# Moving weight pieces, a level table and a few waits in a hand-ordered attention and mixture-of-experts kernel

## The chip, the cores and the metric

The kernel runs on one core of one Trainium2 chip. The metric is the device time of one execution in microseconds (us). A core has five engines that run their own instruction streams and meet only at semaphores: TensorE (PE), VectorE (DVE), ScalarE (ACT), GpSimd (POOL) and SyncE (SP), which here only issues DMAs.

## The reference, cut to what matters

16 batches of 256 tokens of width 256. Each batch goes through a cross attention (16 heads of 16, queries from the normalised `x`, keys and values from a context), and then through a feed-forward part: one shared expert that all tokens take, and two routed experts of which each token takes one with its full weights and the other as a constant level, since an expert that is not chosen sees a zero token.

```
x = x + xattn(layernorm(x), ctx, ctx, Wq, Wk, Wv, Wo)       # x: (16, 256, 256)
x = x + ffn(layernorm(x), gate_w, w1, b1, w2, b2, sw1, sb1, sw2, sb2)

# xattn, for each 64x64 block pair (r, c) with |r - c| <= 3; here 4 blocks of queries and 4 of keys
scores = q_r @ k_c.T * 16 ** -0.5
out_r += softmax(scores) @ v_c                              # a softmax for each block pair, then summed
# ffn, f = layernorm(x)
e = argmax(f @ gate_w.T)                                    # 2 routed experts, hidden width 1024
routing = sum over n of relu((f if n == e else 0) @ w1[n] + b1[n]) @ w2[n] + b2[n]
shared  = relu(f @ sw1 + sb1) @ sw2 + sb2
```

## The kernel before, in words

**Batches and stages.** `iteration(i)` is the same function on every engine. It does the attention of batch `i`, the shared expert of batch `n = i - 1` (called S below, with hidden units u0 to u3: `shared_up`, `shared_down`), and one tile of 256 routed tokens, tile `m = i - 2` (`tile_up`, `tile_down`). Iterations 0, 1 and 2 have no tile yet (`tile` is false), iteration 0 has no shared part. Iterations 4 to 13 or 14 are a loop; after iteration 15 a tail finishes tile 14, the shared part of batch 15, tile 15 (called `last`) and two left-over tiles. Products in full precision are made of a high and a low half of each operand: ACT writes the high half (`..._hi`), DVE or POOL subtracts for the low half (`..._lo`), and PE runs three products.

**Inside an iteration, PE.** Four `visit`s compute scores for row maxima (DVE's `maximum`, line 1176); `maxima` transposes these (line 604) for the shift of the softmax, which SP carries through DRAM into `QP` (`shift`). Then come the next batch's projections: k (from the context's `c_hi`, `c_lo`), the transposes of its tokens, and q. ACT and DVE write q and k into `T`, SP stores them in DRAM (`bounces`) and loads them spread over heads into `KP` and `QP` (`spread`, 24 DMAs in two halves). Eight pairs of heads follow: `scores_t` (line 622), ACT's exponentials, `values` (line 638), and DVE's `divide` (lines 1187 to 1197), which writes `T` and counts `t_done`. `divide` of pair 0 waits until q and k have left `T`. `attention_out` (line 652) sums the blocks; its first half needs pairs 0 to 3 and its second pairs 4 to 7. `visit(i + 1, 0)` (line 589), `project_out` (line 666, result added to the residual `x1` by DVE line 1203), `front_v` (v of the next batch) and `prep_tokens` (line 542, after the second layer norm) end the iteration.

**Weights.** The raw weights of the experts come in 24 pieces of 256 KB, loaded by POOL into 5 staging buffers (`stage`, which lie in buffers that are free in the beginning, two of them `h32`). ACT writes the high half of a piece (`split_high`, line 960), POOL the low half (`split_low`, line 1537) and then loads the next piece that uses this buffer. `SPLITS_AT` says how many pieces are split at each of the numbered places of iteration 0. Pieces 0 to 7 are the shared expert's, 8 to 23 the routed ones'. PE waits for all 24 before iteration 1. `table(e)`, in iterations 1 and 2, computes the constant level of expert `e` out of the whole of it: 24 products.

**Order.** Every engine's order is that of the code. SP is a queue too: a DMA that waits holds back all DMAs behind it. `load_residual(i)` waits for `y_done`, which DVE raises in the middle of the divides (iterations 1 and 2) or at their start (later), and it stands ahead of `spread`.

## Time and profile before

| what | value |
|---|---|
| median of 3 runs | 916.06 us (911.68 to 916.23) |
| the profiled execution, its own time | 914.49 us |
| span of its trace (first to last instruction) | 912.7 us |
| PE busy | 798.9 us (88%) |
| DVE, ACT, POOL busy | 593.8, 497.3, 429.5 us |
| mean granted TensorE clock | 0.954 of full speed |

The span is 1.8 us shorter than the execution's own time. Busy time is an average over very different stages. In the stretch of the weight pieces PE has gaps and runs at a low clock; in the loop it is nearly always busy. In the rows below, a number in square brackets is the idle time of the engine just before the instruction, with what ended it.

### The profile page before, as it was taken

Reading aid. Unit: us, or ns where it says so; the run is one execution under the profiler, and the core shown is the slowest. Engines: PE = TensorE matmul, PEld = TensorE weight load, DVE = VectorE, ACT = ScalarE, POOL = GpSimd, SP = SyncE. Lnnn points to the kernel's source line nnn. Section 1 sums busy time; section 2 is a strip of 40 time slices with the busy share of each in tenths; the row PEclk is TensorE's granted clock in tenths of the full one; section 3 lists DMA queues with packets and bytes.
Section 4 is the critical chain, followed back from the end, with each engine's and each line's share of the span. In section 5 each row is a group of like instructions: output and inputs, shape, how many; then the busy total and the mean of one; then the engine's idle time right before and its main releaser. Section 6 shows DMA issues by size and latency. Waiting matters only on the chain.

```text
span 912.7 us, 24404 instructions
## 1 busy us (share of the span) xinstructions
PE 798.9 (88%) x8374; PEld 665.8 (73%) x8374; DVE 593.8 (65%) x1248; ACT 497.3 (54%) x1150; POOL 429.5 (47%) x780
## 2 busy tenths in 40 slices
PE   3465777788999999999999999999999999989894
PEld 3333756577886869697878788787879697868794
DVE  4457577576757777685858676767677686745331
ACT  2264453636565575746575656556574756465452
POOL 2667333342536364554536363637364554455311
PEclk8576998999999999999999999999999999999997
DMA  6669221263624544544535353444444444414730
GB/s 193 185 194 304 69 86 35 81 206 96 199 79 123 161 138 144 159 141 140 170 115 196 114 166 125 145 140 136 161 128 151 149 144 136 148 49 140 239 109 23
DMA packets 97387, 128.19 MB, mean 140 GB/s; under 512 B 14655, under 2 KB 82623, under 8 KB 97088
## 3 DMA queue, kind: packets, MB, share of 16 engines
q1 hardware_dynamic: 89760, 107.89, 38.4%
q0 software_dynamic: 6624, 18.95, 6.2%
q10 hardware_dynamic: 960, 0.79, 0.4%
q8 instruction: 26, 0.43, 0.2%
q14 instruction: 17, 0.14, 0.1%
HBM read 90.80 MB, written 37.04 MB: 140 GB/s over the span
## 4 chain that ended last, share of the span: by engine, by line
PE 62%; DVE 14%; DMA 9%; issue 4%; ACT 4%; POOL 2%; SPq 2%; ACTq 1%; DVEq 0%; POOLq 0%
PE hid L533 16%; PE acc L724 14%; PE nd L638 11%; PE work L533 6%; PE work L622 5%; DVE nmax L1176 4%; PE work L666 3%; DVE PT L1219 2%; PE work L589 2%; DMA QP<-scratch_m 2%; DVE T L1192 2%; DVE check L1187 1%; DMA scratch_q<-T 1%; PE work L542 1%; DMA scratch_m<-mT 1%
## 5 line engine op out<-in xcount | busy, mean ns | idle before, releaser
L1442 POOL TENSOR_TENSOR hl<-h,hh 128x256 fp32r<-128x256 f32 x228 | 169.0, 744 | 326.1 <-ACT hh L982 325.9
L966 ACT ACTIVATE PT<-work 128x512 f32<-128x512 f32 x192 | 106.3, 605 | 55.6 <-PE work L622 55.5
L1195 DVE RECIPROCAL T<-nd 128x256 f32<-128x256 f32 x51 | 89.4, 1753 | 37.9 <-PE nd L638 32.8
L724 PE MATMUL acc<-w_hi,hh 128*128 128x256 f32 (+1 forms) x528 | 112.5, 295 | 0.0
L982 ACT ACTIVATE h<-hid,bias 128x256 f32<-128x256 f32 x144 | 69.1, 480 | 74.7 <-PE hid L533 74.7
L533 PE MATMUL hid<-Xs,W 128*128 128x256 f32 x816 | 109.6, 288 | 0.2
L533 PEld LDWEIGHTS hid<-Xs,W 128*128 128x128 f32 x816 | 102.9, 195 | 2.6 <-DVE Xs L1129 0.7
L724 PE MATMUL acc<-w_lo,hh 128*128 128x256 f32 (+1 forms) x528 | 104.7, 280 | 0.0
L533 PE MATMUL hid<-Xr,W 128*128 128x256 f32 x768 | 104.1, 285 | 0.0
L533 PEld LDWEIGHTS hid<-Xr,W 128*128 128x128 f32 x768 | 94.1, 188 | 5.1
L638 PE MATMUL nd<-PT,V 128*32 128x256 f32 x1024 | 84.0, 401 | 11.5 <-DVE T L1192 5.3
L1176 DVE TENSOR_REDUCE nmax<-work 128x8 f32<-128x512 f32 x128 | 82.3, 686 | 15.0 <-PE work L589 14.6
L724 PEld LDWEIGHTS acc<-w_hi,hh 128*128 128x128 f32 x528 | 80.6, 189 | 11.0 <-issue 7.0
L724 PE MATMUL acc<-w_hi,hl 128*128 128x256 f32 (+1 forms) x528 | 82.9, 279 | 0.0
L1176 DVE TENSOR_REDUCE nmax<-nd 128x8 f32<-128x512 f32 x128 | 82.8, 680 | 0.0
L724 PEld LDWEIGHTS acc<-w_lo,hh 128*128 128x128 f32 x528 | 81.0, 190 | 0.0
L638 PE MATMUL nd<-PT,bsum 128*32 128x256 f32 x1024 | 80.7, 387 | 0.0
L982 ACT ACTIVATE h<-hid,bsel 128x256 f32<-128x256 f32 x120 | 57.8, 481 | 41.1 <-PE hid L533 39.9
L622 PEld LDWEIGHTS work<-QP,KP 56*128 56x128 f32 x384 | 37.7, 188 | 50.7 <-issue 34.1
L724 PEld LDWEIGHTS acc<-w_hi,hl 128*128 128x128 f32 x528 | 70.9, 189 | 0.0
L982 ACT ACTIVATE hh<-hid,bias 128x256 fp32r<-128x256 f32 x144 | 69.4, 482 | 0.0
L622 PE MATMUL work<-QP,KP 56*128 56x256 f32 x384 | 61.4, 330 | 7.5 <-ACT hh L982 3.7
(191 smaller groups left out, 1651.5 us busy)
## 6 DMA issues: line engine op xcount, KB each, us to landing
W<-w1q SPq DMA_DIRECT2D x64, 512.0 KB, 5.8
KP<-scratch_k SPq DMA_DIRECT2D x192, 64.0 KB, 2.4
QP<-scratch_q SPq DMA_DIRECT2D x180, 64.0 KB, 2.3
scratch_k<-T SPq DMA_DIRECT2D x16, 512.0 KB, 3.5
scratch_q<-T SPq DMA_DIRECT2D x16, 512.0 KB, 3.2
yt<-yq SPq DMA_DIRECT2D x17, 260.0 KB, 2.8
xt<-xq SPq DMA_DIRECT2D x17, 256.0 KB, 3.8
xin<-x SPq DMA_DIRECT2D x16, 256.0 KB, 3.5
```

Source lines behind the costliest of these rows:

```text
L533: mm = nc.tensor.matmul(dst, R(s), R(m), start=n == 0, stop=n == len(steps) - 1)
L589: mm = nc.tensor.matmul(banks[s][:, SEQ * n:SEQ * n + SEQ], R(QP[rows, 2 * g + n, P * t:P * t + P]), R(KP[rows, 2 * g + n, :]), start=True ...
L622: mm = nc.tensor.matmul(banks[s][:, SEQ * t:SEQ * t + SEQ], R(KP[rows, p, P * t:P * t + P]), R(QP[rows, p, :]), start=True, stop=True)
L638: mm = nc.tensor.matmul(nd[r:r + 32, p % 2, kind, :], V[:, t, 2 * p + s, :] if kind == 0 else bsum[:, :], PT[:, (2 * p + s) % 4, t, :], st ...
L666: mm = nc.tensor.matmul(bank[:, D * t:D * t + D], R(part[:, c, P * t:P * t + P]), R(w[:, c, :]), start=first, stop=part is a_lo and c == D ...
L724: mm = nc.tensor.matmul(acc[:, t, :], R(h[:, u % 2, a, P * t:P * t + P]), R(row), start=first, stop=u == UNITS - 1 and h is hl and a == 1, ...
L966: nc.scalar.activation(PT[:, j % 4].rearrange("p t q -> p (t q)"), score_bank(j), ACT.Exp).then_inc(sem["exp_done"], 1)
L982: last = nc.scalar.activation(dst, hid[:, u % 2, a, :], ACT.Relu, bias=bias[:, 2 * u + a:2 * u + a + 1])
L1176: nc.vector.tensor_reduce(nmax[:, t, :].rearrange("q (b s p) -> q s p b", s=2, b=NBLK) [:, s, 2 * g:2 * g + 2, :], bank.rearrange("q (n b ...
L1192: nc.vector.scalar_tensor_tensor(out=T[:, p, :], in0=check[:, p % 2], scalar=2.0, in1=T[:, p, :], op0=ALU.add, op1=ALU.mult).then_inc(sem[ ...
L1195: nc.vector.reciprocal(T[:, p, :], nd[:, p % 2, 1, :]).then_inc(sem["inverted"], 1)
L1442: nc.gpsimd.tensor_tensor(R(hl[:, u % 2, a]), h32[:, u % 2, a], hh[:, u % 2, a], ALU.subtract).then_inc(sem["hl_done"], 1)
```

## The change

These things move, and nothing is computed differently:

1. `context_high(1)` and `context_low(1)` run ahead of the weight pieces, not behind the first four.
2. The split places become (4, 0, 0, 0, 0, 4, 2, 1, 1, 1, 1, 1, 1, 1, 1, 2, 0, 4), the last one in iteration 1. Pieces 20 to 23 are so split in iteration 1, between the shared expert's u1 and u2, and their buffers are 2, 3, 4 and again 3, since `h32` is in use by then. PE waits for pieces 6 and 7 before iteration 1, and for the last piece in `table(0)`.
3. DVE makes the low halves of pieces 5, 7 and 9.
4. `make_constants` goes from before the divides of iteration 0 to behind that of pair 3; `scores_t` of iteration 0 waits for the load of the constants only.
5. In iterations 0 to 2 the residual's load goes behind `spread`.
6. In iterations 1 and 2 `shared_up(n, 3)` goes ahead of the q projection, and `table` behind `front_v`.
7. Everywhere `ranks` goes behind `shared_down(n, 1)`. In iterations 3 to 15 the halves of `attention_out` are apart: the first ahead of `tile_down(m, 1)`, the second behind the first scores of the next batch.
8. Tail: the token load of tile `last` goes behind its second weight load, from behind all four and the bias; `finish_shared` goes ahead of the low half of tile `last`'s u0.

```
-SPLITS_AT = (4, 0, 0, 0, 0, 2, 2, 1, 1, 1, 1, 1, 1, 1, 1, 3, 5)
-SLOTS = [n % STAGES for n in range(W1_PIECES + W2_PIECES)]
+SPLITS_AT = (4, 0, 0, 0, 0, 4, 2, 1, 1, 1, 1, 1, 1, 1, 1, 2, 0, 4)
+ON_VECTOR = (5, 7, 9)
+SLOTS = [n % STAGES for n in range(W1_PIECES + W2_PIECES - 4)] + [2, 3, 4, 3]
...
# SP: load_tile
-                    if u == 0 and not at:
+                    if u == (1 if at else 0):
                         sp.wait_ge(sem["x_queued"], 32 * (m + 1))
                         load_tile_x(m, row)
...
-                if at:
-                    sp.wait_ge(sem["x_queued"], 32 * (m + 1))
-                    load_tile_x(m, row)
...
# SP: iteration
-                if type(i) is int and i == 0:
-                    sp.wait_ge(sem["consts_read"], 1)
-                    load_residual(0, first=True)
-                else:
+                if tile:
                     load_residual(i)
...
                         spread(half)
+                if type(i) is int and i == 0:
+                    sp.wait_ge(sem["consts_read"], 1)
+                if not tile:
+                    load_residual(i, first=type(i) is int and i == 0)
...
# PE: scores_t of iteration 0
-                        pe.wait_ge(sem["consts_read"], 1)
+                        pe.wait_ge(sem["consts_loaded"], 16 * 9)
...
# PE: iteration
                 if shared:
+                    shared_down(n, 1)
                     ranks(n, claim(i, ("rk", 0), tile=tile))
-                    shared_down(n, 1)
...
+                    if shared:
+                        shared_up(n, 3)
                 if more:
                     front_project(i + 1, "q", 0, a_hi, a_lo, "xT_lo", tile=tile)
...
-                elif shared:
-                    shared_up(n, 3)
...
+                attention_out(i, more, 0)
                 if tile:
                     tile_down(m, 1, expert)
-                elif shared:
-                    table(i - 1)
-                attention_out(i, more)
-                if more:
+                    if more:
+                        scores(i + 1, 0)
+                attention_out(i, more, 1)
+                if more and tile:
+                    scores(i + 1, 1)
+                elif more:
                     visit(i + 1, 0)
...
                     front_v(i + 1)
+                if shared and not tile:
+                    table(i - 1)
...
-            pe.wait_ge(*low_done(len(pieces) - 1))
+            pe.wait_ge(*low_done(6))
+            pe.wait_ge(*low_done(7))
...
# ACT: iteration
+                    if u == 1:
+                        splits(i, 17)
...
# DVE: iteration
+                if type(i) is int and i == 0:
+                    split_low(ON_VECTOR[0])
+                    split_low(ON_VECTOR[1])
                 if more:
                     front_q(i + 1)
                 if type(i) is int and i == 0:
-                    make_constants()
+                    split_low(ON_VECTOR[2])
...
# DVE: tail
+            finish_shared(last)
             last_low(tile_unit(last, 0), 0)
-            finish_shared(last)
...
# POOL: iteration
-                if more:
+                splits(i, 17)
+                if more and shared:
                     context_low(i + 1)
```

The instruction order on ACT in the first half of iteration 0, from the fourth weight piece to the q projection's high half (`W` and `w_hi` rows are pieces, `c_hi_t` the context of batch 1, `T` the halves of k and then q, `a_hi_t` the tokens). Before:

```order
L960 ACTIVATE W<-yt 128x2x256
L956 ACTIVATE c_hi_t<-ctx_in 128x512
L929 ACTIVATE mT<-work 128x128
L960 ACTIVATE w_hi<-xt 128x512
L960 ACTIVATE w_hi<-h 128x512
L929 ACTIVATE T<-work 128x512
L929 ACTIVATE a_hi_t<-work 128x512
L960 ACTIVATE w_hi<-h 128x512
L960 ACTIVATE w_hi<-yp 128x512
L929 ACTIVATE T<-work 128x512
```

And now:

```order
L969 ACTIVATE W<-yt 128x2x256
L938 ACTIVATE mT<-work 128x128
L969 ACTIVATE w_hi<-xt 128x512
L969 ACTIVATE w_hi<-h 128x512 x2
L969 ACTIVATE w_hi<-yp 128x512
L938 ACTIVATE T<-work 128x512
L938 ACTIVATE a_hi_t<-work 128x512
L969 ACTIVATE W<-yt 128x2x256
L969 ACTIVATE W<-xt 128x2x256
L938 ACTIVATE T<-work 128x512
```

The context is gone from between the pieces (it stands ahead of the first), and the high half of k stands behind pieces 6 and 7.

POOL at the start of iteration 1 (`hl` are low halves of the shared expert's hidden units, two instructions a unit; `w_lo` pieces; `c_lo_t` the context of batch 2). Before:

```order
L1442 TENSOR_TENSOR hl<-h,hh 128x256 x4
L1427 TENSOR_TENSOR c_lo_t<-ctx_in,c_hi_t 128x512
L1442 TENSOR_TENSOR hl<-h,hh 128x256 x4
L1465 TENSOR_TENSOR own<-ids,rank 128x2
```

And now:

```order
L1462 TENSOR_TENSOR hl<-h,hh 128x256 x4
L1557 TENSOR_TENSOR w_lo<-yp,w_hi 128x512
L1557 TENSOR_TENSOR w_lo<-yt,w_hi 128x512
L1552 DMA yt<-w 128x512
L1557 TENSOR_TENSOR w_lo<-xt,w_hi 128x512
L1557 TENSOR_TENSOR w_lo<-yt,w_hi 128x512
L1447 TENSOR_TENSOR c_lo_t<-ctx_in,c_hi_t 128x512
L1462 TENSOR_TENSOR hl<-h,hh 128x256 x4
```

Four pieces stand ahead of the context, and the load of the last of them is issued only behind the second.

PE in iteration 3 (the loop has the same order, with register instructions in between), from the second product of `tile_down(m, 1)` to the output projection (`T,hsum` is `attention_out`, `KP,QP` the next batch's scores, `hid` is `tile_up(m, 3)`). Before:

```order
L724 MATMUL acc<-w_lo,hh 128x256 x2
L724 MATMUL acc<-w_hi,hl 128x256 x4
L652 MATMUL work<-T,hsum 32x64 x32
L589 MATMUL work<-KP,QP 128x256 x4
L589 MATMUL nd<-KP,QP 128x256 x4
L533 MATMUL hid<-Xr,W 128x256 x12
L666 MATMUL work<-wp_hi,a_hi_t 128x256
```

And now, first the end of `values` and the start of `tile_down`:

```order
L638 MATMUL nd<-PT,V 32x256 x4
L638 MATMUL nd<-PT,bsum 32x256 x4
L652 MATMUL work<-T,hsum 32x64 x16
L725 ISA
L725 MATMUL acc<-w_hi,hh 128x256 x2
```

then from the end of `tile_down`:

```order
L725 MATMUL acc<-w_lo,hh 128x256 x2
L725 MATMUL acc<-w_hi,hl 128x256 x4
L589 MATMUL work<-KP,QP 128x256 x4
L652 MATMUL work<-T,hsum 32x64 x16
L589 MATMUL nd<-KP,QP 128x256 x4
L533 MATMUL hid<-Xr,W 128x256 x12
L667 MATMUL work<-wp_hi,a_hi_t 128x256
```

One half moved up over `tile_down`, and four score matmuls moved up over the other half.

## Rows read from the trace of the kernel before

**Rows 1.** Windows: window, length, busy time of PE, PEld, DVE, ACT, POOL, PEclk, DMA share, GB/s.
```profile
52.00:90.00 38.00, 23.02 (x260) 13.83 (x260) 28.86 (x45) 22.81 (x46) 28.64 (x31) 0.74 0.86 269
396.60:445.33 48.73, 47.03 (x514) 39.31 (x515) 35.03 (x75) 29.31 (x71) 24.77 (x47) 1.00 0.46 145
```

**Rows 2.** Timeline, 36 to 50 us: start, duration, engine, line, instruction; last, line 1532's landing.
```profile
37.66 0.55 POOL L1532 DMA_DIRECT2D yp<-w  x1 [0.30 <-POOL W L1537]
41.80 0.55 PE L533 MATMUL work<-c_hi_t,wp_hi 128*128 128x256 f32 x1 [6.07 <-POOL c_lo_t L1427]
47.05 0.55 PE L533 MATMUL work<-a_hi_t,wp_hi 128*128 128x256 f32 x1 [1.50 <-DVE a_lo_t L1129]
...
DMA to landing us min/median/max: 3.4/3.4/3.4
```

**Rows 3.** Timeline, 52 to 91 us.
```profile
52.39 0.59 PE L622 MATMUL work<-QP,KP 56*128 56x256 f32 x5 [2.43 <-DVE bias L1294]
...
74.16 1.27 DVE L1192 SCALAR_TENSOR_TENSOR T<-check,T 128x256 f32<-128x256 f32 x1
...
80.55 0.69 DVE L1203 TENSOR_TENSOR x<-work,x 128x512 f32<-128x512 f32 x1 [1.82 <-PE work L666]
...
83.40 2.61 DVE L1149 TENSOR_SCALAR xhat<-x,mv,rstd 128x256 f32<-128x256 f32 x2
...
90.03 0.80 PE L589 MATMUL work<-KP,QP 48*128 48x256 f32 x4 [2.79 <-POOL w_lo L1537]
```

**Rows 4.** Timeline of iteration 1, 97 to 142 us.
```profile
98.01 1.30 POOL L1427 TENSOR_TENSOR c_lo_t<-ctx_in,c_hi_t 128x512 fp32r<-128x512 f32 x1
...
103.03 0.36 PE L533 MATMUL work<-c_hi_t,wp_hi 128*128 128x256 f32 x1
...
108.26 1.56 PE L533 MATMUL hid<-Xs,W 128*128 128x256 f32 x12
...
114.88 1.76 DVE L1195 RECIPROCAL T<-nd 128x256 f32<-128x256 f32 x1 [5.10 <-DMA scratch_q<-T]
...
126.28 0.37 SPq L317 DMA_DIRECT2D x<-x  x1
...
137.93 0.69 DVE L1203 TENSOR_TENSOR x<-work,x 128x512 f32<-128x512 f32 x1 [0.58 <-PE work L666]
...
140.87 0.74 DVE L1149 TENSOR_SCALAR xhat<-x,mv,rstd 128x256 f32<-128x256 f32 x2
...
141.71 0.41 PE L542 MATMUL work<-id,xhat 128*128 128x128 f32 x2 [2.40 <-issue]
```

**Rows 5.** Waits of the whole span: waiter, waited for, total us, times, longest.
```profile
PE work L693 <- DVE mask L1230: 10.8, 14, 1.3
...
PE work L652 <- DVE T L1192: 9.9, 14, 2.3
```

**Rows 6.** Timeline of a loop iteration, 405 to 427 us.
```profile
407.17 0.69 DVE L1176 TENSOR_REDUCE nmax<-nd 128x8 f32<-128x512 f32 x1
...
408.37 0.27 PE L604 MATMUL work<-id,nmax 128*128 128x128 f32 x1
...
423.56 2.77 SPq L305 DMA_DIRECT2D QP<-scratch_q  x6
```

**Rows 7.** Timeline of the tail, 855 to 872 us.
```profile
855.82 0.38 SPq L370 DMA_DIRECT2D xt<-xq  x1
...
859.22 1.12 PE L542 MATMUL work<-id,xt 128*128 128x128 f32 x4 [2.88 <-DMA xt<-xq]
...
864.14 0.39 SPq L370 DMA_DIRECT2D xt<-xq  x1
...
867.02 0.50 PE L764 MATMUL acc<-level,level_row 128*128 x2 [1.54 <-DVE yp L1257]
...
871.60 0.60 PE L542 MATMUL work<-id,xt 128*128 128x128 f32 x4
```

**Rows 8.** Tile xt, 863 to 866 us: issue to landing of the one DMA there.
```profile
DMA to landing us min/median/max: 6.7/6.7/6.7
```

More of the change, by code:

```diff
@@ L227, in low_done @@
         def low_done(n):
-            return sem["stage_lo"], n + 1
+            return (sem["stage_lo_dve" if n in ON_VECTOR else "stage_lo_pool"],
+                    sum((m in ON_VECTOR) == (n in ON_VECTOR) for m in range(n + 1)))
         def slot_pieces(k):
@@ L641, in values, with attention_out @@
                 mm.then_inc(sem["pv_done"], 1)
-            def attention_out(i, more):
-                bank = claim(i, ("at", 0), more).rearrange("p (c t) -> p c t", c=DC)
-                for c in range(DC):
-                    pe.wait_ge(sem["t_done"], PAIRS * i + 4 * c + 4)
-                    for r in range(NBLK):
-                        queries = slice(BLOCK * r, BLOCK * r + BLOCK)
-                        for q in range(4):
-                            mm = nc.tensor.matmul(bank[32 * q:32 * q + 32, c, queries], hsum[:, r, :],
-                                                  T[:, 4 * c + q, queries], start=True, stop=True)
-                mm.then_inc(sem["at_full"], 1)
+            def attention_out(i, more, c):
+                bank = claim(i, ("at", 0), more) if c == 0 else work[:, BANK["at", 0], :]
+                bank = bank.rearrange("p (c t) -> p c t", c=DC)
+                pe.wait_ge(sem["t_done"], PAIRS * i + 4 * c + 4)
+                for r in range(NBLK):
+                    queries = slice(BLOCK * r, BLOCK * r + BLOCK)
+                    for q in range(4):
+                        mm = nc.tensor.matmul(bank[32 * q:32 * q + 32, c, queries], hsum[:, r, :],
+                                              T[:, 4 * c + q, queries], start=True, stop=True)
+                if c == DC - 1:
+                    mm.then_inc(sem["at_full"], 1)
             def project_out(i, more):
@@ L770, in table @@
                 pe.wait_ge(sem["y_done"], e + 1)
+                if e == 0:
+                    pe.wait_ge(*low_done(len(pieces) - 1))
                 for h, parts, ready in ((hh, (w2_hi, w2_lo), "table_relu"), (hl, (w2_hi,), "table_lo")):
@@ L1015, in splits @@
             def splits(i, k):
-                if type(i) is int and i == 0:
+                if type(i) is int and i == (k == 17):
                     for n in slot_pieces(k):
@@ L1028, in iteration @@
                         level_high(i - 2)
-                if more and not shared:
-                    context_high(i + 1)
+                    if u == 1:
+                        splits(i, 17)
                 high(i, "mT_full", work[:, BANK[("mT", 0)], 0:P], mT[:, 0, :], "mT_hi")
@@ L1039, in iteration @@
                     tile_high(m, work_bank("xr"))
+                elif shared:
+                    shared_relu(n, UNITS - 1)
                 splits(i, 6)
@@ L1045, in iteration @@
                     tile_relu(m, 1)
-                elif shared and not tile:
-                    shared_relu(n, UNITS - 1)
                 exps(i, 0)
@@ L1095, in _ @@
             front_v(0, acc[:, :, :])
+            context_high(1)
             for n in slot_pieces(0):
@@ L1286, in level_low, with split_low @@
                                         ALU.subtract).then_inc(sem["level_made"], 1)
+            def split_low(n):
+                dve.wait_ge(sem["stage_hi"], n + 1)
+                _, hi, lo = pieces[n]
+                nc.vector.tensor_tensor(R(lo), stage(n, lo), hi, ALU.subtract).then_inc(sem["stage_lo_dve"], 1)
             def make_constants():
@@ L1334, in iteration @@
                         finish_shared(n)
+                    if type(i) is int and i == 0 and p == 3:
+                        make_constants()
                 if norm1:
@@ L1536, in split_low @@
                 _, hi, lo = pieces[n]
-                nc.gpsimd.tensor_tensor(R(lo), stage(n, lo), hi, ALU.subtract).then_inc(sem["stage_lo"], 1)
+                nc.gpsimd.tensor_tensor(R(lo), stage(n, lo), hi, ALU.subtract).then_inc(sem["stage_lo_pool"], 1)
             def split_and_load(n):
-                split_low(n)
+                if n not in ON_VECTOR:
+                    split_low(n)
                 if SLOTS[n] in SLOTS[n + 1:]:
@@ L1550, in splits @@
             def splits(i, k):
-                if type(i) is int and i == 0:
+                if type(i) is int and i == (k == 17):
                     for n in slot_pieces(k):
@@ L1610, in _ @@
                 load(n)
+            context_low(1)
             for n in slot_pieces(0):
```

4 lines of the change are left out of this document (2 added, 2 removed).

## The prediction

> **What bounds the kernel now.** I read the windows first. In the loop an iteration takes 48.73 us with PE busy for 47.03 of them at a granted clock of 1.00, so what can go there is 1.7 us of gaps; while the weight pieces are split, PE is busy for 23.02 of 38 us and the clock is 0.74 [rows 1]. So a us of gap costs more than itself at the start, and in the loop each small gap counts twelve or thirteen times. The list of waits names the loop's two gaps, DVE's mask and DVE's last T [rows 5]. Then I followed the timeline by stage: which wait ends last, and what it waits for.
>
> **The start, to the first shared matmuls of iteration 1 (step A).** The k projection of batch 1 stood idle for 6.07 us, until 41.80, for the context's low half, which POOL ran behind four pieces [rows 2]. Ahead of the pieces that half is ready near 31 and k starts at 35.7. But ACT's high half of k now stands behind piece 7, whose load is issued at 37.66 and takes 3.4, so lands at 41.1 [rows 2]: split 0.6, high half of k 0.6, of the tokens 0.6, and DVE's low half of them 0.7 give 43.7 for the q projection, before 47.05. That is 3.2 of the 6.07; the rest is late by the piece. The first transposed scores waited 2.43 more for the constants' sum [rows 3]; that goes, and the next thing late is q's way through DRAM, which frees T: about 3.9 us earlier than before. The constants then stand among the divides, 1.0 us of DVE, and DVE's three pieces are beside PE's q projection. With the 1.2 us which the first guess waited and no longer does, the last T (before at 74.16 + 1.27 = 75.4 [rows 3]) comes at 72.0, 3.4 earlier.
>
> From T the residual was 5.1 later, at 80.55 [rows 3]: now 77.1. Its load is now issued behind 24 spreads, at about 71, and lands by 75.5: hidden, by 1.6 us. The second norm's scaling took 2.61 beside POOL's pieces [rows 3] and 0.74 in iteration 1, where POOL was free [rows 4]; four pieces fewer follow now, so 1.9 goes. PE then also had to wait for the last pieces until 90.03 [rows 3]; now it goes on when the tokens are transposed, at 82.0. **A = -8.0.** Ends: -9.5 (the constants cost nothing, POOL gets done earlier) and -5 (pieces 8 and 9 hold up q's high half by 3).
>
> The row of 2.61 against 0.74 is DVE and POOL at the same time. The Trainium skill (SBUF — State Buffer, "SBUF: two separate sides") says that an exclusive lock on a shared port pair makes one of the two wait for the whole of the other's instruction, also where a DVE operation has two SBUF inputs. The trace agrees. By that rule the moved constants, which ran free, wait behind a piece's low half each, and A would be up to 2 us smaller; this speaks against that edit, and lies within A's ends.
>
> **Iteration 1 (step B).** POOL's context for batch 2 ran at 98.01, and k started at 103.03 [rows 4], with slack. Now four pieces are ahead: two low halves (2.6), the issue of piece 23's load (0.3 + 0.55, landing 3.4 later as in [rows 2]: 104.3), its high half 0.6, low half 1.3, context 1.3: 107.5. PE's k is late by 4.4, and ACT's shift and third relu wait behind piece 23 as well. The move of u3 ahead of q fills the gap in which PE waited for the tokens' low half, but only takes 1.56 from behind it [rows 4]; DVE's first divide, at 114.88 for q's bounce of 5.10 [rows 4], comes 4.0 later, as the bounce has less beside it. **B = +4.0.** Ends: +1 (PE had gaps at the clock's low level behind it that shrink) and +8 (a load of 8 us as when DRAM is busy).
>
> **Ends of iterations 1 and 2 (step C).** The table stood between values and the block sum, and SP's spreads stood behind the residual's load, which went at 126.28 when y was done [rows 4]. Now the spreads go as the scores do, done by then, and PE runs block sum, next scores, projection, v as soon as T is there: residual 3.0 earlier. Then the table, 24 products at 0.13 (1.56 / 12 [rows 4]) = 3.1, fills what was the wait of 2.40 for the norm at 141.71 [rows 4], and becomes the last: 139.3 + 3.1 - 3.0 = 139.4. **2.3 each, C = -4.6.** The residual's load is now issued 5.6 behind the last transposed scores and lands 1 us ahead of need; if it does not, C loses 1 to 2 each. In iteration 2 nothing is in the way of the context, and u3's relus are done before the exponentials: -0.4. Ends of C: -7 (both residuals' whole gain) and -1.
>
> **Loop (step D).** The mask's wait is 10.8 us in 14 [rows 5], about 0.70 in a loop iteration. Behind `shared_down` the ranks find the mask ready. But the transposition of the maxima follows at 408.37, and DVE's last maximum ends at 407.17 + 0.69 = 407.86 [rows 6] whatever PE does, since DVE is busy from the second scores on: PE gets 0.40 of 0.70, and then waits for the maximum. In iterations 1 and 2 PE waits for it anyway: 0. 13 x 0.40 = 5.2. The block sum's wait for T is (9.9 - 2.3) / 13 = 0.58 [rows 5]; now four score matmuls of about 0.34 in all come before the second half too, and T does not move: 12 x 0.34 = 4.1 (iteration 15 has no next scores). The cover of ACT's and DVE's halves behind the sum gets 0.34 shorter, with over 0.5 left. What is queued behind the sum, scores and `tile_up`, is only earlier. **D = -9.3.** Ends: -15.5 (both gaps whole, 1.28 x 12) and 0 (the period is DVE's and the DMAs').
>
> **Tail (step E).** Tile `last`'s tokens were loaded at 855.82, PE waited 2.88 until 859.22 [rows 7]. The load waits for the scatter of tokens, whose data are in line with 2 MB of weights. Half of these now come behind: scatter done at about 853, tokens at 856.4 when PE asks, 2.9 less, 1.4 more since PE does not fall to the low clock, and DVE's y, for which PE waited 1.54 at 867.02 [rows 7], goes too: PE would be 5.8 earlier at 871.60. But the next tile's tokens are issued at 864.14 by SP after a fixed run of DMAs and land 6.7 later, at 870.8 [rows 7, 8]. SP gets only 1.5 to 2 earlier: about 869.2. PE waits there for 3.3, and its clock falls there instead (1.4, of the 2.4 left). 871.6 - 869.2 - 1.4 = 1.0, and I take half of it. **E = -0.5.** Ends: -5.8 and +1.5.
>
> Here a rule speaks against the edit. The Trainium skill (DMA: Bandwidth & Descriptors, "Queues, rings and completion order") says that a DMA engine takes turns between the queues it has work for, packet by packet. By that rule the scatter, on POOL's queue, does not stand behind all of SP's weights, the tokens come no earlier, and the next ones 1.4 later: E = +0.6, and the whole 1.1 more. No row here separates the two; it is a case below.
>
> **Sum.** -8.0 + 4.0 - 4.6 - 0.4 - 9.3 - 0.5 = -18.8. Against the profiled execution's own 914.49 (its span is 912.7): 895.7. That execution is 1.6 below the median of the runs; I take 896.
>
> **Rivals.**
> - *DVE keeps the period.* PE gets earlier at two places, and waits at the next for the same DVE work: D = 0. For: the maximum ends only 0.5 ahead of PE [rows 6]. Against: DVE is busy 35.03 of 48.73 [rows 1], and each of its chains starts at a PE product. -9.5: 905. Chance 0.13.
> - *The pieces cost more in iteration 1.* The load of piece 23 takes 8 us beside the stores of W1 that are then under way, ACT and PE stand: B = +8, and A at its small end: 901 to 904. For: the whole order of ACT stands behind it. Against: the DMAs were near idle there. 0.12.
> - *The packets take turns*: 897. 0.05, inside the forecast's range.
> - *More than reckoned*: both loop gaps go whole, and the tail's token load for the next tile keeps pace: -6.2 - 5.3: 884. 0.07.
> - *It does not do what it says*: in A the moved splits hold ACT by as much as the context gained, B is +8, D 0: within 912 to 920. 0.05.
> - *Slower.* One mechanism: in the loop the next scores stand ahead of the second half of the block sum, so a late spread of q holds the output projection and all behind it. Its last issue ends at 423.56 + 2.77 = 426.3 [rows 6], the scores come at 435.5. From a landing over 9.2 us after this it costs its whole lateness in twelve iterations; for slower than 920.6 it must be 2 us late in each. 922. Against: the slack. 0.05, with what I overlooked.
>
> The forecast has the rest, 0.58 with the packets' case, own range 889 to 902. A measurement tells about 0.5% from no change: 911.5 to 920.6. Faster by more: 0.90; within: 0.05; slower: 0.05. The range for 8 in 10 reaches to DVE's case and nearly to the large one: 886 to 907.
>
> **What would show it.** A: k of batch 1 starts near 36, q near 44, iteration 1's second scores near 82. B: PE waits about 4 for the context before k of batch 2. C: x1's load behind the spreads, no wait for it, table last before the transposes. D: no wait for the mask, a new one of about 0.3 at line 604's transposition for the maximum, the period 48.0. E: PE's wait for tokens is at the next tile's. A period still at 48.7, or over 8 us of idle PE in the first half of iteration 1, would make it wrong.

## The result and the profile after

The changed kernel takes 904.30 us (median of 4 runs, 903.63 to 906.78), the kernel before 915.99 (911.68 to 916.23): a ratio of 0.9886, 95% interval 0.9855 to 0.9916, so 11.7 us faster. I had forecast 896, 20 us faster. The direction was right, and 904.30 lies in the range of 886 to 907, but outside the 889 to 902 of the forecast's own case: the gain was little over half of the size forecast. The profiled execution is the slowest of the four, 906.78 with a span of 905.0; a second set of runs of the same kernel (below) has 905.00, ratio 0.9882, with nearly the same stages.

The stages are cut where the prediction cut them: the second scores of iteration 1 (PE, KP,QP), its first divide (DVE, RECIPROCAL), the second scores of iteration 3, the residual of batch 15 (DVE, `x<-work,x`), and the end of the last instruction that a timeline row shows. Behind that, the span has 8.7 us more before and 9.0 after.

| stage | before | forecast | changed | changed, again |
|---|---|---|---|---|
| A: start to 90.03 | 90.03 | -8.0 | -5.6 | -4.5 |
| B: to the first divide of iteration 1 | 24.85 | +4.0 | +3.8 | +3.7 |
| C: to the second scores of iteration 3 | 81.36 | -5.0 | -0.4 | -0.4 |
| D: to the residual of batch 15 | 635.11 | -9.3 | -10.3 | -10.2 |
| E: to the end | 72.66 | -0.5 | +4.4 | +4.4 |
| sum | 904.01 | -18.8 | -8.0 | -7.0 |

The forecast of C is the -4.6 and the -0.4 of the prediction's sum together. B and D came near to the forecast. A lacks 2.4, C lacks 4.6, and E lost 4.4 where I had a half gained. The sum of -8.0 is less than the -11.7 of the medians, since the profiled execution before is 1.5 below its median and the changed one 2.5 above.

**Start.** The timeline of the changed kernel (start, duration, engine, line, instruction, idle time before it and what ended it):

```profile
36.79 0.56 PE L533 MATMUL work<-c_hi_t,wp_hi 128*128 128x256 f32 x1
...
44.76 0.55 PE L533 MATMUL work<-a_hi_t,wp_hi 128*128 128x256 f32 x1 [4.21 <-DVE a_lo_t L1139]
...
47.59 0.50 PE L622 MATMUL work<-QP,KP 56*128 56x256 f32 x4
...
63.59 0.21 DVE L1306 CAST before<-xhat 128x128 bf16<-128x128 f32 x1
63.73 0.41 DVE L1307 TENSOR_TENSOR bias<-bias,x 128x256 f32<-128x256 f32 x1
64.17 1.66 DVE L1309 TENSOR_TENSOR bias<-bias,xhat 128x256 f32<-128x256 f32 x1
65.76 1.75 DVE L1205 RECIPROCAL T<-nd 128x256 f32<-128x256 f32 x1
...
73.43 1.26 DVE L1202 SCALAR_TENSOR_TENSOR T<-check,T 128x256 f32<-128x256 f32 x1
...
80.14 0.69 DVE L1213 TENSOR_TENSOR x<-work,x 128x512 f32<-128x512 f32 x1 [1.82 <-PE work L667]
...
83.00 0.73 DVE L1159 TENSOR_SCALAR xhat<-x,mv,rstd 128x256 f32<-128x256 f32 x2
...
84.43 0.50 PE L589 MATMUL work<-KP,QP 48*128 48x256 f32 x4
```

k started at 36.8 and not at 41.80 [rows 2], q at 44.8 (forecast 43.7), the transposed scores at 47.6 and not at 52.39 [rows 3]. The 4.8 us won there were down to 0.7 at the last T (74.69 in place of 75.43) and 0.4 at the residual (80.55 before [rows 3]). Between them stand the constants, 2.2 us of DVE, whose last addition takes 1.66 beside POOL's pieces, where before it took 0.42 with POOL idle:

```profile
51.82 0.42 DVE L1294 TENSOR_TENSOR bias<-bias,xhat 128x256 f32<-128x256 f32 x1
```

What was forecast behind the residual came: the scaling takes 0.73 and not 2.61 [rows 3], and PE waits for no piece.

**Iteration 1.**

```profile
95.17 0.59 POOL L1552 DMA_DIRECT2D yt<-w  x1 [0.30 <-POOL w_lo L1557]
...
98.30 0.63 ACT L969 ACTIVATE w_hi<-yt 128x512 fp32r<-128x512 f32 x1 [5.36 <-DMA yt<-w]
...
100.22 1.26 POOL L1447 TENSOR_TENSOR c_lo_t<-ctx_in,c_hi_t 128x512 fp32r<-128x512 f32 x1
...
101.64 0.55 PE L533 MATMUL work<-c_hi_t,wp_hi 128*128 128x256 f32 x1 [3.25 <-POOL c_lo_t L1447]
...
113.11 1.76 DVE L1205 RECIPROCAL T<-nd 128x256 f32<-128x256 f32 x1 [3.22 <-DMA scratch_q<-T]
```

k of batch 2 came 17.2 after the second scores (17.5 forecast, 13.0 before), behind the last piece, whose load took 3.1, and the context.

**Ends of iterations 1 and 2.** PE in iteration 1:

```profile
126.54 0.63 PE L652 MATMUL work<-T,hsum 128*32 128x64 f32 x32
...
129.89 1.08 PE L652 MATMUL work<-T,hsum 128*32 128x64 f32 x32 [2.72 <-DVE T L1202]
...
130.90 0.80 PE L589 MATMUL work<-KP,QP 48*128 48x256 f32 x4
...
134.29 1.06 PE L667 MATMUL work<-wp_hi,a_lo_t 128*128 128x256 f32 x4
...
139.83 0.38 PE L542 MATMUL work<-id,xhat 128*128 128x128 f32 x2
```

And windows (columns as in [rows 1]), first before, then after. The first covers the same four us of the trace in both, not the same instructions; the second is the first half of iteration 2, from its second scores to its first divide; the third is its end, from the first divide to iteration 3's second scores.

```profile
130.00:134.00 4.00, 2.77 (x77) 2.28 (x76) 2.50 (x7) 0.32 (x1) 2.25 (x3) 1.00 0.59 182
...
142.42:168.79 26.37, 20.06 (x155) 17.53 (x155) 13.80 (x32) 11.40 (x28) 8.65 (x16) 0.88 0.21 61
168.79:196.24 27.45, 21.42 (x284) 15.10 (x283) 21.80 (x43) 13.06 (x26) 10.79 (x22) 1.00 0.34 98
```

```profile
130.00:134.00 4.00, 3.71 (x47) 3.24 (x48) 2.63 (x8) 0.60 (x1) 0.91 (x2) 0.50 0.56 167
...
140.36:163.95 23.59, 17.38 (x154) 15.22 (x154) 13.76 (x31) 11.56 (x28) 10.03 (x22) 0.99 0.22 65
163.95:194.10 30.15, 25.15 (x284) 19.22 (x284) 21.83 (x44) 13.04 (x26) 9.38 (x16) 0.84 0.53 167
```

Without the table in front of it PE stands 2.72 us before the block sum's second half. Right behind, the granted clock is 0.50, the lower level: the four products with `a_lo_t` take 1.06 and not 0.63. At the end of iteration 2 the same 284 products keep PE busy 3.7 us longer. In iteration 1 the residual comes at 135.38 (137.93 before [rows 4]): 22.27 after the first divide, where it was 23.05.

Stage C is the sum of three stretches. The end of iteration 1 took 27.25 (27.54 before), the first half of iteration 2 23.59 (26.37 before), and the end of iteration 2 30.15 (27.45 before). So the ends gained 0.3 and lost 2.7, and what hides the loss in the sum is the first half of iteration 2, 2.8 shorter: PE is busy 2.7 us less in it, at a granted clock of 0.99 and not 0.88. The low spell of the clock that stood there before now stands in the ends.

**Loop.** One iteration, the answer to the second window of [rows 1], and the waits of the whole span that answer to [rows 5]:

```profile
389.62:437.76 48.14, 47.50 (x516) 39.67 (x516) 35.02 (x75) 29.25 (x71) 24.78 (x47) 1.00 0.47 147
```

```profile
PE work L652 <- DVE T L1202: 12.3, 16, 2.7
...
PE work L604 <- DVE nmax L1186: 7.2, 5, 2.3
```

Ten periods, from the residual of batch 4 to that of batch 14, take 480.46 us: 48.05 each, before 48.72, forecast 48.0. No wait for the mask is left in the list. The wait for T has a larger total, but 8.1 of it are three waits of 2.7 at the ends of iterations 0, 1 and 2; in a loop iteration it is 0.28 or 0.29. The new wait that I expected at line 604, for the maximum, does not occur in the loop (the 5 of the list are in iterations 0 to 4): the gain stops at the maximum without an idle time that shows.

**Tail.** SP and PE:

```profile
836.26 0.97 POOL L1525 DMA_INDIRECT xq<-xhat,pos  x1 [0.30 <-issue]
...
842.72 0.38 SPq L372 DMA_DIRECT2D xt<-xq  x1
...
843.29 0.85 SPq L368 DMA_DIRECT2D W<-w1q  x2
...
845.50 0.66 PE L542 MATMUL work<-id,xt 128*128 128x128 f32 x4 [1.59 <-DMA xt<-xq]
...
848.78 0.37 SPq L488 DMA_DIRECT2D yq<-T  x1
...
850.86 1.82 SPq L368 DMA_DIRECT2D W<-w1q  x4
...
853.70 0.39 SPq L372 DMA_DIRECT2D xt<-xq  x1
...
860.98 1.12 PE L542 MATMUL work<-id,xt 128*128 128x128 f32 x4 [5.33 <-DMA xt<-xq]
...
875.74 0.60 PE L542 MATMUL work<-id,xt 128*128 128x128 f32 x4
```

Before, the scatter's last issue and PE's transposition of the last tile's tokens were:

```profile
848.72 0.97 POOL L1505 DMA_INDIRECT xq<-xhat,pos  x1 [0.30 <-issue]
...
883.67 0.60 PE L542 MATMUL work<-id,xt 128*128 128x128 f32 x4
```

The token load, which waits for the scatter, is issued 6.5 us after the scatter's last issue, with two weight loads ahead of the tokens; before it was 7.1 with four (848.72 to 855.82). PE's wait at tile `last` goes from 2.88 [rows 7] to 1.59. But the next tile's tokens, 4.92 behind PE's first transposition before (859.22, 864.14 [rows 7]), are now issued 8.20 behind it, and PE stands 5.33. Then its clock falls: from there to the last tile's transposition it takes 14.76 at a granted clock of 0.80, before 12.07 at 1.00 (871.60 to 883.67).

### The profile page after: what moved, and what is told of

The parts are those of the page before. It is cut to its first block, busy times and chain, and to the rows that moved or that the text cites. A ratio compares the mean times of both kernels' runs of the same rounds, so it can differ in the third digit from the quotient of the medians.

```text
span 905.0 us, 24405 instructions
## 1 busy us (share of the span) xinstructions
PE 808.0 (89%) x8374; PEld 675.4 (75%) x8374; DVE 592.0 (65%) x1251; ACT 496.4 (55%) x1150; POOL 424.9 (47%) x777
## 4 chain that ended last, share of the span: by engine, by line
PE 59%; DVE 15%; DMA 12%; issue 4%; ACT 4%; POOL 2%; SPq 2%; ACTq 1%; DVEq 0%; POOLq 0%
PE hid L533 15%; PE acc L725 12%; PE nd L638 12%; PE work L622 5%; PE work L533 5%; DVE nmax L1186 4%; DMA QP<-scratch_m 3%; PE work L667 3%; DMA scratch_m<-mT 2%; DVE PT L1229 2%; DVE T L1202 2%; DMA scratch_q<-T 2%; DVE check L1197 2%; DVE T L1205 2%; PE work L589 1%
```

## The experiments

Each run lists its ratio to the kernel before, timed beside it, with a 95% interval of some 0.3% (3 us) either way. Two versions are compared by these ratios, and differences of 3 us are at the edge of what they tell; the stages of the traces carry the argument there. The edits are to the changed kernel, alone where nothing else is said.

**1. The changed kernel again.**

> The changed kernel once more, unaltered. Its profiled execution (906.8 us) was the slowest of its four (903.6 to 904.9 otherwise). If what I read there is the kernel, not that one execution: 904 to 906, the tail from batch 15's residual to the end again near 86.1 us against 81.4 of before, and the loop's period again 48.1. If the tail's loss was that execution's own: tail 82 to 83 and total near 904 or below.

Measured: 905.00 us, ratio 0.9882 (0.9855 to 0.9910). Its profiled execution has the tail at 77.07, as the first, and ten periods at 480.17. (The expectation's 86.1 and 81.4 count to the end of the span; the table's tail ends at the last row: 77.07 and 72.66.) What the trace showed is the kernel, the tail's loss included.

**2. Tail.**

```
# SP: load_tile, back as before
+                    if u == 0 and not at:
...
+                if at:
+                    sp.wait_ge(sem["x_queued"], 32 * (m + 1))
+                    load_tile_x(m, row)
```

> Only the token load of tile `last` goes back behind its four weight loads and the bias; finish_shared stays ahead of the low half of u0. Theory (SP's queue): the load between the weights came only 0.7 us earlier against batch 15's residual, but put two weight loads, the bias and the stores of zero rows behind a wait, so the next tile's tokens came 2 later, PE stood 5.3 us and its clock fell: undone, 4 to 5 us less than the changed kernel (near 900), PE's wait for tokens about 2.9 at `last` and under 1 at the next tile. Rival (finish_shared did it, or the stream of weights): no change within 1 us. Rival (one execution's own): 0 to 1 us.

Measured: 901.90 us, ratio 0.9846 (0.9816 to 0.9876), 3 less than the kernel again; in the trace the tail is 72.65, 4.4 less. The tail of the changed kernel's code is not one number: it took 75.06 to 77.80 in the nine executions traced that have it, 76.5 in the mean, so the loss is some 2.4 to 5.1 against the one trace before.

```profile
840.28 0.38 SPq L372 DMA_DIRECT2D xt<-xq  x1
...
848.61 0.39 SPq L372 DMA_DIRECT2D xt<-xq  x1
...
855.90 0.66 PE L545 MATMUL work<-id,xt 128*128 128x128 f32 x4 [1.56 <-DMA xt<-xq]
```

PE waits 2.64 and 1.56 at the two tiles in place of 1.59 and 5.33. SP's queue it was. `finish_shared` ahead is neither a loss nor a gain in these two traces (72.65 and 72.66): PE's wait for y is gone, and the tokens of the next tile are what PE waits for next.

**3. Constants.**

```
# DVE: iteration 0
                     split_low(ON_VECTOR[2])
+                    make_constants()
...
-                    if type(i) is int and i == 0 and p == 3:
-                        make_constants()
```

> Only make_constants of iteration 0 goes from behind the divide of pair 3 to directly behind DVE's split of piece 9, ahead of the divides, where DVE stood 3.2 us for q's way through DRAM. PE's first transposed scores still wait for the constants' load alone. Theory (constants among the divides cost 2.3 us of DVE, 1.66 of it the last addition beside POOL, and the last T is late by it): last T 2 to 2.5 us earlier, residual 77.5 to 78.3 in place of 80.1, total 2 to 4 less than the changed kernel, since the stretch runs at the low clock. Rival (PE's values, late by the low clock, or the exponentials behind pieces set the last T): 0 to 0.7 less.

Measured: 900.57 us, ratio 0.9838 (0.9801 to 0.9875), 4.4 less than the kernel again and a little more than the 2 to 4 expected.

```profile
52.01 1.92 DVE L1309 TENSOR_TENSOR bias<-bias,xhat 128x256 f32<-128x256 f32 x1
```

The addition is as slow, but DVE waited there anyway. The residual comes at 77.30 (I had forecast 77.1), the second scores at 81.59 (82.0). The start differs between executions, the second scores of iteration 1 by up to 4.5 us (81.05 to 85.51 in the eight whose code is the same up to there), so I take the span from the first transposed scores to the last T in all 13 executions traced: 24.8 to 27.4 in the nine with the constants among the divides, 23.8 to 24.2 in the four with them ahead, 2.1 less in the mean. Before, it took 23.0, so some 1 us beside the constants is not explained.

**4. Table back.**

```
# PE: iteration
+                if shared and not tile:
+                    table(i - 1)
                 attention_out(i, more, 0)
...
-                if shared and not tile:
-                    table(i - 1)
```

> Only the level table of iterations 1 and 2 goes back from behind the values' projection to before the block sum. Theory (the table at the end is what took back the gain: PE waits 2.7 for the last T, its clock falls to the low level, projection and v run at it, and the table then stands between the residual and the tokens' transposes): the ends of iterations 1 and 2 get 1 to 2 us shorter each, total 2 to 4 less. Rival (as I forecast: the move itself is worth 2.3 a time and the loss lies elsewhere): 3 to 5 more. Third: 0 within 1, the two places cost the same.

Measured: 905.21 us, ratio 0.9890 (0.9864 to 0.9917): no difference. The ends are 1.0 and 1.4 us shorter (first divide to next second scores: 26.23 against 27.24 and 28.70 against 30.11), but the stretches between them are longer (25.23 against 23.66): the clock is 0.95 in the second end and 0.92 behind the first, where the changed kernel has 0.84 and 0.99. The third expectation held, and neither place is good: one leaves a gap of 2.7 before the sum, the other one of 2.4 before the tokens' transposes, for the norm.

**5. and 6. Ranks, halves.**

```
# PE: iteration, ranks back
+                    ranks(n, claim(i, ("rk", 0), tile=tile))
                     shared_down(n, 1)
-                    ranks(n, claim(i, ("rk", 0), tile=tile))
```

> Only the ranks' products go back ahead of shared_down(n, 1), in all iterations. Theory (as forecast: PE gets 0.40 of the mask's 0.70, the maximum takes the rest): the loop's period goes from 48.08 to 48.45 to 48.50, PE waits for the mask again 0.7 a time, total 5 to 6 more than the changed kernel in its own call. Rival (both gaps count whole): 0.7 each, 9 more. Rival (DVE keeps the period, the gain of the period came from the halves): 0 to 1 more.

```
# PE: iteration, halves together
                     tile_down(m, 1, expert)
-                    if more:
-                        scores(i + 1, 0)
+                attention_out(i, more, 0)
                 attention_out(i, more, 1)
...
+                if more:
+                    visit(i + 1, 0)
```

> Only the halves of attention_out stand together again behind tile_down(m, 1), and the next batch's first scores behind both; all iterations. Theory: the second half starts when T comes, whatever stands before it; what was gained is the part of the wait that four score products fill, read as 0.24 a period (0.61 less the ranks' 0.37), not my 0.34: the period 48.30 to 48.35, total 3 to 3.5 more. In iterations 1 and 2 nothing. Rival (0.34 as forecast): 4 to 4.5 more. Rival (0.59, the whole wait): 7 more.

Measured: 910.85 us, ratio 0.9956 (0.9932 to 0.9979), and 907.16 us, ratio 0.9915 (0.9881 to 0.9949). Ten periods take 484.68 and 482.46: 0.42 and 0.20 more each than the changed kernel's 480.46. PE, first with the ranks back, then with the halves together:

```profile
403.61 0.16 PE L694 MATMUL work<-mask,before 128*128 128x2 bf16 x1 [0.72 <-DVE mask L1240]
...
434.51 0.65 PE L652 MATMUL work<-T,hsum 128*32 128x64 f32 x32 [0.30 <-DVE T L1202]
```

```profile
430.29 0.65 PE L652 MATMUL work<-T,hsum 128*32 128x64 f32 x32 [0.58 <-DVE T L1198]
```

The mask's 0.72 give 0.42, the halves fill 0.3 of the wait for T and give 0.20. Together that is 0.62 of the 0.68 that the period lost, so the two nearly add up; no run undoes both.

The ranks matter outside the ten periods too. With them back, the stretch from the second scores of iteration 3 to the residual of batch 4 takes 98.44, as before (98.18); it takes 94.76 to 96.46 in the twelve other executions of changed kernels.

**7. Pieces back.**

```
-SPLITS_AT = (4, 0, 0, 0, 0, 4, 2, 1, 1, 1, 1, 1, 1, 1, 1, 2, 0, 4)
+SPLITS_AT = (4, 0, 0, 0, 0, 4, 2, 1, 1, 1, 1, 1, 1, 1, 1, 2, 4, 0)
-SLOTS = [n % STAGES for n in range(W1_PIECES + W2_PIECES - 4)] + [2, 3, 4, 3]
+SLOTS = [n % STAGES for n in range(W1_PIECES + W2_PIECES)]
...
-            pe.wait_ge(*low_done(6))
+            pe.wait_ge(*low_done(len(pieces) - 1))
```

> Pieces 20 to 23 are split at the end of iteration 0 again, in their old buffers, and PE waits for all before iteration 1; the context ahead of the pieces and DVE's three pieces stay. Theory (the move pays in iteration 0 what it costs in iteration 1, as forecast for B at 4): the second scores of iteration 1 come 4 to 5 later, the first divide of iteration 1 is within 1 of the changed kernel's, total -1 to +1.5. Rival (moving them was what made the start faster): 3 to 5 more. Rival (it only costs): 2 to 4 less.

Measured: 905.40 us, ratio 0.9898 (0.9863 to 0.9933): the same. From the residual of batch 0 to the second scores it takes 8.06 in place of 4.29, 3.8 more; from there to the first divide of iteration 1 24.49 in place of 28.68, 4.2 less. So the move pays in iteration 0 what it costs in iteration 1, and the whole is a draw. The second scores themselves come only 1.6 later than in the changed kernel's profile, as the residual was 2.2 earlier in this execution.

**8. Residual's load back.**

```
# SP: iteration
-                if tile:
+                if tile or i in (1, 2):
                     load_residual(i)
```

> On the changed kernel only SP's load of the residual goes back ahead of the spreads in iterations 1 and 2. Theory (as forecast: the spreads wait behind it for y, and PE's next scores wait for q): the next scores come behind a wait for q of 1 to 2, and the ends of iterations 1 and 2 get 1 to 2 longer, total 1 to 4 more than the changed kernel. Rival (PE waits 2.7 for T there anyway and the clock is low behind it either way, so this order is hidden): 0 to 0.7 more.

Measured: 907.50 us, ratio 0.9934 (0.9910 to 0.9957), some 0.5% over the changed kernel's 0.9886 and 0.9882. PE's waits in iteration 1, then in iteration 2:

```profile
PE work L589 <- DMA QP<-scratch_q: 3.1, 1, 3.1
```

```profile
PE work L589 <- DMA QP<-scratch_q: 2.2, 1, 2.2
```

The end of iteration 1 is 30.22 and not 27.25; that of iteration 2 only 0.25 longer, as PE is at the high clock more of it (0.89, not 0.84). This part of the edit is worth about 3 in the trace; the ratios say 4 to 5.

**9. The table cut in two.** `table(e, part)` runs its 16 products with `hh` or its 8 with `hl`:

```
                 attention_out(i, more, 0)
...
+                if shared and not tile:
+                    table(i - 1, 0)
                 attention_out(i, more, 1)
...
                 if shared and not tile:
-                    table(i - 1)
+                    table(i - 1, 1)
```

> On the changed kernel only the level table is cut in iterations 1 and 2: 16 products between the halves of the block sum, 8 where the table stands. Theory (what the changed order gained at the ends of iterations 1 and 2 went into a spell of the low clock that PE's 2.7 of idle time before the second half set off): the granted clock of the projection behind stays nearer 1.00, the span from iteration 2's second scores to iteration 3's falls from 53.8 to about 51, iteration 1's by 1 to 2, total 3 to 5 less than the changed kernel's 905. Rival (in the version with four edits that span fell since everything before was earlier, not by the cut): 0 to 1 less.

Measured: 897.16 us, ratio 0.9837 (0.9795 to 0.9878). PE in iteration 2, and the window from its first divide to iteration 3's second scores:

```profile
175.84 0.65 PE L652 MATMUL work<-T,hsum 128*32 128x64 f32 x32 [0.75 <-DVE T L1206]
...
178.99 0.63 PE L667 MATMUL work<-wp_hi,a_lo_t 128*128 128x256 f32 x4
```

```profile
159.00:184.00 25.00, 20.12 (x275) 14.02 (x273) 21.72 (x43) 13.05 (x26) 9.60 (x16) 1.00 0.55 167
```

The gap is 0.75 and not 2.72, the clock stays at 1.00, the products take 0.63, and the end takes 25.00 in place of 30.15. From its second scores to iteration 3's, iteration 2 takes 49.98; it took 53.82 before and 53.74 in the changed kernel. One execution proves less than the median: in all traces that span is 50.0 to 51.2 in the four with the cut (9., 10. twice, 11.), and 53.6 to 53.9 in five of the seven that have the changed kernel's order there, but 51.5 and 52.1 in the other two (6., halves together, and 7.), whose ends had a clock of 0.94 and 0.88 behind the same gap of 2.7. The means are 50.8 and 53.2. Iteration 1 gains as well (52.97, not 55.93), though in 2. it took 53.55 without the cut. Over the whole of stage C the two groups do not meet: 75.8 to 77.0 with the cut, 78.9 to 82.6 in the seven without, 76.3 and 80.8 in the mean. The ratio is 0.5% below the changed kernel's, which is the same 4.5 us, but on its own it would prove little, as the intervals just overlap.

What the cut saves at the end of iteration 2 is the time of the products and not idle time: PE is idle for 4.9 of the 25.00 and for 5.0 of the 30.15. It is busy 20.1 to 22.2 in the four with the cut, and 24.9 to 25.2 in those five of the seven, 21.4 and 22.7 in the other two.

**10. Four edits together,** timed twice: 2 and 3 above, the cut table, and in the tail

```
                 load_w1(W1[:, 0], 0, u, "w1_again")
-            sp.wait_ge(sem["padded"], 64)
-            sp.wait_ge(sem["xr_full"], FIRST_LEFT - 1)
-            load_tile_x(FIRST_LEFT, rows[0])
+                if u == 0:
+                    sp.wait_ge(sem["padded"], 64)
+                    sp.wait_ge(sem["xr_full"], FIRST_LEFT - 1)
+                    load_tile_x(FIRST_LEFT, rows[0])
```

> Four edits on the changed kernel: the token load of tile `last` back behind its weights, the next tile's tokens loaded behind the first of the four weight loads that follow and not behind all, the constants ahead of the divides, and the level table cut: its 16 products with the high hidden half between the halves of the block sum, where PE waited 2.7 for T, its 8 others where the table stands now. Theory: 4.4 of the tail, 0.5 to 1 for the earlier tokens, 2.5 of the constants, and 0.5 to 1 in each of iterations 1 and 2, since no gap is left long enough for the clock to fall: 895 to 897, against 905. Rival for the table (the low spell of the clock only moves into the next half iteration, as between before and after, where the span from iteration 2's second scores to iteration 3's was 53.82 and 53.74): 897 to 899.

> The version with four edits once more, to stand beside the one with the last piece moved and to see how far single executions differ: 891 to 894, iteration 2's second scores to iteration 3's again about 51, the tail again about 71 from batch 15's residual to the end.

Measured: 892.11 us, ratio 0.9761 (0.9727 to 0.9796), and 893.21 us, ratio 0.9778 (0.9742 to 0.9813). By the ratios that is some 10 to 11 us below the changed kernel, more than the 8 to 10 I expected for the first. It is about the sum of the three edits alone (by their ratios 3, 4 and 4). The tail is 71.02 and 70.80:

```profile
840.79 0.39 SPq L372 DMA_DIRECT2D xt<-xq  x1
...
847.72 0.60 PE L546 MATMUL work<-id,xt 128*128 128x128 f32 x4
```

The next tile's tokens, with one weight load ahead, land after 3.8 us and not 7.2, and PE does not wait. Iteration 2 takes 50.87 and 51.22.

**11. The last piece,** on top of these four:

```
+SLOTS = [n % STAGES for n in range(W1_PIECES + W2_PIECES - 4)] + [2, 3, 4, 2]
...
# POOL
                     context_low(i + 1)
+                splits(i, 18)
```

> On the version with four edits: the last piece goes into the buffer of piece 20 and not of piece 21, so its load is issued behind one low half and not two, and POOL makes the context's low half before the last piece's; ACT splits it behind the shift's high half. Theory (iteration 1's 4 us are the context behind four pieces, and ACT's third relu behind the last load): k of batch 2 comes 2 to 3 earlier against the second scores, the first divide 1.5 to 2.5, total 1 to 2.5 less than the version without (892). Rival (the maximum, at 98.1 in the changed kernel, and the clock set that place): 0 to 0.7 less. Rival (the last low half now comes too late for the table): 0 to 1 more.

Measured: 890.39 us, ratio 0.9749 (0.9714 to 0.9784), the fastest median of all, but its interval covers both of the four edits' alone. In its trace the first divide comes 29.28 behind the second scores, and 26.85 and 29.82 without it: nothing is told apart. Open.

## Why the prediction was right in direction and wrong in size

**A, short by 2.4.** The step that failed is "The constants then stand among the divides, 1.0 us of DVE". They took 2.2, as the addition took 1.66 beside POOL's pieces, and they stand on the chain that sets the last T. Measured: 2.1 us between the means of the two sets of executions in 3. The prediction weighed a rule of the Trainium skill (SBUF — State Buffer, "SBUF: two separate sides"), by which the constants could cost up to 2 more beside a piece's low half, and left it out of the sum. One of the three operations waited: in twelve of thirteen executions the addition ends 0.28 to 0.30 behind the end of POOL's subtraction beside it. By that rule the trace agrees in the wait; by the same passage the instruction that starts first has the ports, and there the trace does not agree, as the subtraction's row starts 0.08 to 0.35 behind the addition's.

The constants were priced 1.1 too low, and that is half of the shortfall. The rest of A has errors that partly cancel. The sum for the last T does not come out (3.9 - 1.0 + 1.2 is 4.1 earlier, not the 3.4 used), the transposed scores came 4.8 earlier and not 3.9, and from there to the last T it took some 1 us more than before even with the constants ahead. That experiment 3 meets the last T, the residual and the second scores within 0.6 of the forecast is so in part luck: the forecast had 1.0 of constants in them. A's size is uncertain as well. In the eight executions that share this start, A is -4.5 to -9.0, in the mean -6.1, all against one trace before.

**B, right:** +3.8 for +4.0, by the chain that the forecast names: four pieces, then the context, then k. In the eleven executions with this order it is +2.0 to +5.0, in the mean +3.5. Its rival, a load of 8 us, fell: 3.1.

**C, short by 4.6, the largest error with E.** The step that failed is "PE runs block sum, next scores, projection, v as soon as T is there: residual 3.0 earlier". The ends of iterations 1 and 2 came at -0.3 and +2.7 in place of -2.3 each, 7.0 too much together; the first half of iteration 2, forecast at -0.4, came at -2.8 and hid 2.4 of that. The order of the waits was right, but I priced what follows at the high clock, though the wait for T, which the table filled before, was now a bare gap of 2.72 at PE. The residual came 0.8 earlier in iteration 1 and 1.2 later in iteration 2, both against the first divide. Experiment 9 shows it: with most of the gap filled and nothing else changed, stage C is 4.5 shorter in the mean, iteration 2 by 2.4, and the kernel is some 0.5% faster. With the cut, C is at -4.4 to -5.6 against the one trace before, about the -5.0 that the forecast had for it without the cut. When the clock falls behind such a gap, and for how long, differs from one execution to the next and stays open. The part that I credited to the residual's load is real (experiment 8).

**D, right:** the mask gives 0.42 (0.40 forecast), the halves 0.20 (0.34), and the ten periods 6.8 of the 10.3. The last iteration gave only 0.1, and the other 3.4 are in iterations 3 and 4. Those two took 94.76 us from second scores to the residual of batch 4, before 98.18; two periods' gain is 1.4 of these 3.4. The granted clock there was 1.00 and not 0.96 in the first part, but that is not all: the kernel again had 0.96 there too and took 95.19. With the ranks back it took 98.44, so in one execution the place of the ranks accounts for these iterations as well; why it is worth more there than in the loop stays open. That D as a whole is near its forecast is in part luck.

The rival that DVE keeps the period fell: the period is 48.05. It and the rival of dearer pieces had forecast 905 and 901 to 904, nearer to the measured time than my 896, but both by a mechanism that did not take place.

**E, wrong in sign, short by 4.9.** The step that failed is "Half of these now come behind: scatter done at about 853". With half of the weights moved behind it the scatter was 0.6 us faster, not 3. All traces bear this out: from the scatter's last issue to the token load it takes 6.4 to 6.7 in the nine with two weight loads ahead, and 7.1 to 7.5 in the five with four. That is what the rival in which the packets take turns said of the scatter, and by that rule of the Trainium skill (DMA: Bandwidth & Descriptors, "Queues, rings and completion order") the trace agrees. But the rival reckoned only 0.6 lost: neither it nor my sum saw that SP then issues two weight loads, the bias and the zero rows later, behind its wait, and that these hold the next tile's tokens: 8.20 behind PE's first transposition in place of 4.92, and 2.0 later from the residual of batch 15. That order is SP's own and could have been read beforehand.

## What to carry to other kernels

A wait that a filler job hides is not gone when the job is moved: price the work behind it at the lower clock too, and if the job can be cut, put one part in each gap. A DMA that waits is paid by all that its queue issues later, so write down what stands behind it before moving it ahead. A job moved into an engine's critical chain costs what it takes beside its new neighbours, not what its row showed alone.

## What the runs showed of the hardware

- The granted clock was 0.50 in the four us behind PE's gap of 2.72. Behind a gap of 0.75 it was 1.00 in one execution's iteration 2; in the three others with the cut table the same end had 0.93, 0.96 and 0.97. The same gap did not always end alike: the end of iteration 2 with its gap of 2.7 had 0.83 or 0.84 in five executions, 0.88 and 0.94 in two more with the same order there.
- DVE's addition of 128x256 with two SBUF inputs took 0.42 alone (kernel before), and 1.65 to 1.93 in twelve of the thirteen executions of the changed kernels, in which it stands among POOL's low halves; in the thirteenth (experiment 11) 0.42, though the subtraction beside it starts 0.35 behind it there, and 0.34 behind it in experiment 3, where it took 1.92. What decides it stays open.
- The load of 256 KB of tokens for the next tile took 7.2 us behind four weight loads of 512 KB on its queue (6.4 to 8.2 in the eleven executions with four), and 3.7 or 3.8 behind one in the three executions that have it so.
- The time to the second scores of iteration 1 differs by up to 4.5 us between executions with the same code up to there (81.05 to 85.51), the loop's ten periods by 0.9 at most (479.79 to 480.71 in the eleven executions whose loop is the changed kernel's).
